# Normalising the token rows of the last mixture on VectorE instead of ScalarE, with the second batch's transposes and gate matmuls moved to earlier units

## The reference

```python
x = x + _L1_attn_ref(_layernorm(x, axis=-1), L1_attn_Wq, ...)     # 8 heads over 4 kv heads, causal
x = x + _L1_ffn_ref(_layernorm(x, axis=-1), L1_ffn_scale, ...)

def _L1_ffn_ref(x, scale, gate_w, gate_b, mlp1_w, mlp1_b, mlp2_w, mlp2_b):
    t = x * rsqrt(mean(x * x, axis=-1) + EPS) * scale
    g = einsum('bth,eh->bte', t, gate_w) + gate_b          # 16 experts
    vals, idx = top_k(g, 4); w = softmax(vals)
    ...                                                    # every expert: up, swiglu, down
    acc = acc + r[..., None] * y
    return x + acc
```

## Time and profile before

| | us |
|---|---|
| median of 3 runs (lowest, highest) | 965.39 (965.29, 967.6) |
| the profiled execution's own time | 965.39 |
| its span (first to last instruction) | 963.0 |
| TensorE matmul busy | 897.1 (93%) |
| VectorE busy | 723.9 (75%) |
| ScalarE busy | 623.2 (65%) |
| GpSimd busy | 361.0 (37%) |
| mean granted TensorE clock, share of full speed | 0.975 |

### The profile page before, as it was taken

How to read it: one execution, slowest core, us unless ns; L and a number is a source line. 1 busy time by engine, 2 the same in 40 slices (tenths; PEclk the granted TensorE clock), 3 DMA queues, 4 the chain that set the end, 5 groups by cost and what they waited for, 6 DMA issues and landing times.

```text
span 963.0 us, 17523 instructions
## 1 busy us (share of the span) xinstructions
PE 897.1 (93%) x6208; PEld 582.9 (61%) x6208; DVE 723.9 (75%) x1492; ACT 623.2 (65%) x1259; POOL 361.0 (37%) x401
## 2 busy tenths in 40 slices
PE   3689999999999999999799999999999999999998
PEld 1312222322222232455698889988988899889897
DVE  7799999999999998668655554555465556697877
ACT  3268888888888888544755556565655555465765
POOL 5700000000000010121676769386929693157422
PEclk9779999999999999899799999999999999999999
DMA  2410111111000000000000000000000003000000
GB/s 68 147 46 24 35 52 40 41 37 30 23 19 25 18 1 18 1 1 18 1 1 1 1 17 2 2 1 17 1 1 2 1 1 88 1 1 12 12 12 12
DMA packets 23373, 20.09 MB, mean 21 GB/s; under 512 B 5176, under 2 KB 17440, under 8 KB 23288
## 3 DMA queue, kind: packets, MB, share of 16 engines
q1 hardware_dynamic: 23288, 18.99, 6.7%
HBM read 14.26 MB, written 4.59 MB: 20 GB/s over the span
## 4 chain that ended last, share of the span: by engine, by line
PE 63%; DVE 22%; POOL 7%; issue 4%; ACT 2%; DMA 1%; DVEq 0%; SPq 0%; POOLq 0%; ACTq 0%
DVE halves L842 15%; PE a_sum L2246 9%; PE summed L1056 7%; PE m_down L2502 6%; PE score_bank L1043 5%; PE a_turn L2231 4%; PE max_bank L1003 4%; PE max_bank L1016 3%; PE a_scores L1746 3%; PE a_scores L1748 3%; PE a_scores L1747 3%; POOL a_crossed L1838 2%; POOL a_rotated L1840 2%; PE m_hid L2320 2%; PE m_hid L2321 2%
## 5 line engine op out<-in xcount | busy, mean ns | idle before, releaser
L967 ACT ACTIVATE probs<-score_bank 128x512 f32<-128x512 f32 x512 | 267.8, 601 | 74.3 <-PE score_bank L1043 74.1
L842 DVE TENSOR_REDUCE halves<-max_bank 128x2 f32<-128x1024 f32 x256 | 298.6, 1219 | 10.4 <-PE max_bank L1003 8.3
L2246 PE MATMUL a_sum<-a_v,a_turned 128*128 128x128 f32 x1152 | 165.4, 281 | 2.4 <-ACT a_turned L2106 1.5
L1773 ACT ACTIVATE a_probs<-a_scores,a_lowest 128x896 f32<-128x896 f32 (+7 forms) x128 | 94.9, 742 | 105.4 <-DVE a_lowest L1768 104.7
L2246 PEld LDWEIGHTS a_sum<-a_v,a_turned 128*128 128x128 f32 x1152 | 145.7, 193 | 3.5 <-ACT a_turned L2106 2.1
L1003 PE MATMUL max_bank<-k_stack,q_stack 48*128 48x512 bf16 x512 | 117.2, 397 | 24.9 <-DVE halves L842 24.8
L1056 PE MATMUL summed<-probs,v_tile 128*32 128x512 f32 x1024 | 138.6, 614 | 0.0
L1043 PE MATMUL score_bank<-q_stack,k_stack 50*128 50x512 bf16 x512 | 132.3, 385 | 3.4 <-ACT probs L967 2.2
L1768 DVE TENSOR_REDUCE a_lowest<-a_scores 128x1 f32<-128x896 f32 (+7 forms) x128 | 96.3, 755 | 31.2 <-PE a_scores L1750 30.3
L765 POOL COPY v_tile<-values 128x128 f32<-128x128 f32 x16 | 4.7, 296 | 302.8 <-PE summed L1056 302.6
L1003 PEld LDWEIGHTS max_bank<-k_stack,q_stack 48*128 48x128 bf16 x512 | 25.2, 93 | 123.5 <-DVE halves L842 112.0
(11 more groups left out here) (344 smaller groups left out, 1624.4 us busy)
## 6 DMA issues: line engine op xcount, KB each, us to landing
rope<-in_rope SPq DMA_DIRECT2D x8, 256.0 KB, 3.1
rope<-in_L_ffn_mlp_w SPq DMA_DIRECT2D x8, 256.0 KB, 4.8
q_parts<-l_q_parts SPq DMA_DIRECT2D x2, 768.0 KB, 4.7
k_parts<-l_k_parts SPq DMA_DIRECT2D x2, 768.0 KB, 6.8
q_stack<-q_parts SPq DMA_DIRECT2D x30, 48.0 KB
k_stack<-k_parts SPq DMA_DIRECT2D x30, 48.0 KB
x<-in_L_attn_x SPq DMA_DIRECT2D x2, 512.0 KB, 4.3
q_stack<-shift SPq DMA_DIRECT2D x64, 2.0 KB
```

Of the source, the lines that this page charges most:

```text
L842: dve.reduce_max(halves[:, u % 2, half, :].rearrange("p (x t) -> p x t", x=2)[:, :, qt], max_bank[place % RING][:, :, :], AX_X).then_inc(f ...
L967: act.activation(probs[:, step % PROBS, x, :], score_bank[e % SCORES][:, :], ACT.Exp, scale=SCALE0).then_inc(prob_ready, 1)
L1773: act.activation(probs[:, k % 2, c, 0:row_width(n)], row_of(n), ACT.Exp, bias=lowest[:, n % 8:n % 8 + 1], accum_out=weight[:, k % 4, c:c + ...
L2246: last_use = pe.matmul(sum_bank[:, c * P:(c + 1) * P], turned[:, m % SLOTS, i * P:(i + 1) * P], v[:, b, first + i, q, :], start=(first + i ...
```

## The change

In the attention part the eight rows of batch 0 are normalised by VectorE (`normalise`, a tensor_scalar of the mean and the inverse root) at the same steps of the sequence, `rows 0` and `turn 0`. The offset and its semaphore are gone. GpSimd's two waits for the rows are gone, and groups 1, 2 and 3 of `split_up` stand at `root 1`, `turn 0` and `turn 1` of its sequence. In the mixture the two transposes and the two `lower` steps come one unit earlier, and the gate matmuls are spread one tile a unit over n = 20 to 27 instead of two tiles a unit over n = 22 to 25.

```diff
-        self.offset = sb("m1_offset", [P, TB])
...
-    def find_offset(self, dve, b):
-    def scale_row(self, act, x, tile):
...
on_gpsimd, body:
-                    if n == ("root", 0):
+                    if n == ("root", 1):
                         split_up(1)
-                    if n == ("root", 1):
+                    if n == ("turn", 0):
                         split_up(2)
                     if n == ("turn", 1):
-                        pool.wait_ge(mix_normed, 2)
                         split_up(3)
...
                     if what == "close":
                         b, _, half = BLOCKS[n]
-                        if last and n == NB // B:
-                            pool.wait_ge(mix_normed, 1)
...
on_vector, mix:
                 if step == "root" and i == 2:
-                    m1.find_offset(dve, 0).then_inc(mix_offset, 1)
                     chain.after(m1.find_second_root(dve, chain, 0))
+                if step == "rows" or step == "turn" and i == 0:
+                    c = 0 if step == "rows" else 1
+                    for tile in range(QB * c, QB * (c + 1)):
+                        last = m1.normalise(dve, t.x, tile)
+                    last.then_inc(mix_normed, 1)
...
on_scalar, body:
-                    if what == "mix" and (n[0] == "rows" or n == ("turn", 0)):
-                        if n[0] == "rows":
-                            act.wait_ge(mix_offset, 1)
-                        c = 0 if n[0] == "rows" else 1
-                        for tile in range(QB * c, QB * (c + 1)):
-                            last_row = m1.scale_row(act, t.x, tile)
-                        last_row.then_inc(mix_normed, 1)
...
layer1_mixture:
-        TURN_AT, LOWER_AT = {15: 2, 19: 3}, {16: 2, 20: 3}
-        GATE_AT = {22 + i: range(TB + 2 * i, TB + 2 * i + 2) for i in range(TB // 2)}
+        TURN_AT, LOWER_AT = {14: 2, 18: 3}, {15: 2, 19: 3}
+        GATE_AT = {20 + i: TB + i for i in range(TB)}
...
                 if n in GATE_AT:
-                    for tile in GATE_AT[n]:
-                        gate(tile)
+                    gate(GATE_AT[n])
```

More of the change, by code:

```diff
@@ L438, in normalise @@
                                     self.inverse[:, b, 1, k:k + 1], ALU.subtract, ALU.mult)
-    def find_offset(self, dve, b):
-        return dve.scalar_tensor_tensor(out=self.offset[:, :], in0=self.both[:, b * TB:(b + 1) * TB, 0], scalar=-1.0,
-                                        in1=self.inverse[:, b, 1, :], op0=ALU.mult, op1=ALU.mult)
-    def scale_row(self, act, x, tile):
-        b, k = divmod(tile, TB)
-        return act.activation(self.normed[:, tile, :], x[:, tile, :], ACT.Identity, scale=self.inverse[:, b, 1, k:k + 1],
-                              bias=self.offset[:, k:k + 1])
     def add_input(self, engine, x, tile):
@@ L1664, in layer1_attention @@
         mix_asked, mix_given = sem("mix_asked"), sem("mix_given")
-        mix_offset = sem("mix_offset")
         LAST = KV1 - 1
```

## The result

The changed kernel takes 970.91 us (median of 6 runs, 969.53 to 972.38), the kernel before 965.34 us (6 runs, 963.95 to 967.6). The ratio is 1.0057, 95% interval 1.004 to 1.0074: slower by 3.9 to 7.1 us. The forecast was 970.1 us.

The account below looks back on a forecast made before the run. The prediction took TensorE, with 63% of the chain that ended last, as the bound and asked where it waits. 1.9 + 1.3 + 1.55 = 4.75 us on 965.39 us gave 970.1 us, range 967.4 to 973.0.

Parts of the forecast that it names:

- The attention part: Around 825 us: stall of 2.7 us less 0.81 us of old waits, net +1.9 us, bounds -0.81 and +2.2.
- The stall before `turn (5, 4)`: VectorE's root chain waits for GpSimd's SBUF reads; copy of `turn (5, 2)`, and TensorE with it, 2.7 us late.
- the case named as 2.35: Root chain: one small instruction slips between GpSimd's CAST and TENSOR_TENSOR, so the copy is 2.35 us late, not 3.0.
- old waits: TensorE's waits before two pairs of transposes, 0.50 and 0.31 us, go once VectorE makes the rows: 0.81 us saved.
- The first transpose: Mixture, batch 1, n = 15 to 14: TensorE waits for the rows of n = 11 and 12, +1.3 us.
- The first gate matmul: Mixture, n = 20, one unit after `lower` in n = 19: TensorE waits for `lower`, +1.55 us.
- The spread gate matmuls: Mixture: TensorE visits the 24 gate matmuls eight times instead of four; cost taken as 0, bounds 0 and 0.9 us.
- that case: Rival: TensorE's clock falls during the stall at 823 us, 2.2 us more, 972.3 us; chance 0.18.
- the chain slips through: Rival, attention part: root chain escapes GpSimd, only the rows collide; 967.4 to 969.1, middle 968.3 us; chance 0.18.
- A missing stall in the mixture: Rival: event order around n = 11 to 20 shifts, one mixture stall is absent; 968.7 us; chance 0.12.
- the other side: Rival: GpSimd does not get in VectorE's way and both mixture tables are early enough; 964.6 us; chance 0.07.

Follow-up runs that it names:

- e1: Changed kernel with GpSimd's two waits and the old places of the weight splits put back: ratio to the kernel before 1.002.
- e4: Kernel before with only GpSimd's two waits removed and the weight splits moved, rows still on ScalarE: ratio 1.0047, attention stretch +3.67 us.
- e7: e3 with `close 4` on GpSimd no longer waiting for the first rows: ratio to the kernel before 0.999, attention stretch 16.25 us.
- e9: e3 plus a GpSimd memset of an unused 128x1024 tile beside the root chain: 964.65 us, ratio to the kernel before 0.9984.
- e10: e3 plus a 128x1024 GpSimd copy from SBUF to SBUF beside the root chain: 964.26 us, ratio to the kernel before 0.9978.
- e3: Kernel before with only the rows moved from ScalarE to VectorE and the offset gone, GpSimd's waits kept: ratio 0.9985, attention stretch -0.92 us.
- e5: Kernel before with only the mixture's transposes and `lower` one unit earlier, gate matmuls unmoved: ratio 1.0012, mixture stretch +1.23 us.
- e6: Kernel before with only the gate matmuls spread one tile a unit from n = 21 to 28: ratio 1.0017, mixture stretch +1.56 us.
- e8: Changed kernel with the unused 0.17 us offset instruction put back on VectorE before the second root: ratio to the kernel before 1.0065.

## Why the prediction was right

*The attention part, +1.9 forecast, +1.53 measured.* The stall before `turn (5, 4)` was put at 2.7 us, the middle of two cases; it was 2.30 us, the case named as 2.35, in which one small instruction slips through between a CAST and its TENSOR_TENSOR. e1 and e4 show that it comes with GpSimd's missing waits and moved splits, whoever normalises the rows; e7 shows that one GpSimd instruction is enough for one wait, and e9 and e10 that it is GpSimd's reads. The 0.81 us of old waits came back: 0.77 us here, and 0.84 us in e3, where GpSimd is held.

*The first transpose, +1.3 forecast.* +1.23 us in e5, where it stands alone. *The first gate matmul, +1.55 forecast.* +1.56 us in e6, and 2.64 to 2.91 us for both together in the four kernels that have the whole table (2.85 forecast). These two could be read to a tenth because both are distances: from a fixed event to a place in TensorE's order. *The spread gate matmuls, 0 forecast:* no more than 0.2 us, which is within the scatter of that stretch.

*The rivals.* The clock stayed at full speed in the changed kernel, so that case did not come true; in e8, with one small instruction more, the clock fell. Its price, put at 1.7 to 2.9 us, was about 1.6 us. That the prediction gave this case the smaller chance was right here, but its two reasons, a wait shorter than 3.7 us and dense matmuls on both sides, hold in e4 and e8 too, where the clock fell. That the chain slips through is excluded by VectorE's timeline: its second instruction was issued 0.03 us after GpSimd's start here, 0.03 to 0.05 us after it in e4, e7, e8 and e10, and was held all five times. A missing stall in the mixture and the other side are excluded by the waits of 1.09 and 1.41 us.

*The sum.* 4.75 us forecast, 4.23 us in the two stretches, 5.6 us between the medians with an interval of 3.9 to 7.1 us. What may lie between 4.23 and 5.6 us, the runs don't resolve; the profiles show a spread of 3.5 us in where the first mark falls. It does not come back in every kernel: in e8 the stretches add up to 6.55 us and the medians differ by 6.45 us. So the mechanism and its terms were right, the sum 0.5 us too high, most of it the stall's 2.7 us; that 970.1 us lies within 0.8 us of the measured median is also luck, since the medians lie further apart than the two stretches explain.

## What to carry to other kernels

A wait that seems to hold an engine back for nothing may be keeping it off another engine's critical chain: before it is taken away, look at what will run beside the work it guarded, and whether both read SBUF. A chain of tiny awaited VectorE instructions with two SBUF inputs can pay once per GpSimd instruction that reads SBUF beside it, whatever its own size. Where TensorE is dense, a table of places must keep the distance in time from the event that releases each of them, not only the order; each of the two distances that the change cut by one unit of 1.59 us cost 1.2 to 1.6 us.

## What the runs showed of the hardware that was not expected

TensorE's clock fell to 1.2 GHz after both waits of 3.05 us (e4, e8), about 1.0 us after TensorE had started again, and stayed at 2.4 GHz after the wait of 2.50 us (after), all at the same place between dense matmuls. So a stall can have a second price, larger than what was added to it: with one instruction of 0.17 us more, 0.55 us more of waiting went together with 2.14 us. What decides whether the clock falls stays open, since at 77 us a wait of 1.99 us left it alone and waits of 1.69 to 1.77 us did not.

GpSimd's back-to-back instructions let a waiting VectorE instruction in at each border: the waits end at 824.34, 824.89 and 826.24, one per GpSimd instruction, which is why a chain of four could be held three times. Only in the gap of 0.08 us between the CAST and its TENSOR_TENSOR did a second one get through behind it, and which one that is (L430 in the changed kernel, the offset in e4 and e8) set the stall to 2.50 or 3.05 us.
